# Moving the sum of the query rotation from VectorE to POOL in an attention and feed-forward kernel

## The chip, the cores and the metric

The kernel runs on one core of one Trainium2 chip. The metric is the device time of one execution in microseconds (us). Engines are called as in the profile: PE (TensorE), DVE (VectorE), ACT (ScalarE), POOL (GpSimd), SP (SyncE, which here only issues DMAs).

## The reference

Two sublayers, on an input of 2 batches, 1024 tokens and 512 features in float32:

```
q, k, v = projections of layernorm(x)          # 16 query heads, 4 key/value heads of 128
q = q * cos + rotate_half(q) * sin             # k too
q, k = elu(q) + 1, elu(k) + 1
state += k v^T ; z += k ; out = (q state) / (q z + 1e-6)     # causal linear attention
x = x + layernorm(out @ Wo.T)
h = silu(x' Wg) * (x' Wu), of each group of 4 only the 2 largest by size
x = x + layernorm(h @ Wd)                      # x' = layernorm(x)
```

What matters here is the second line: the rotated query is a sum of two products, `q * cos` and `rotate_half(q) * sin`.

## The kernel before

Every matrix is split into a high part (rounded to the matmul's format) and a low part (the rest), and every product of matrices is three matmuls: high by high, low by high, high by low (`three`, L383 to 386). ACT writes the high parts, and mostly POOL, at times DVE, the low parts by one subtraction. On POOL these all go through the helper `lo` and so have one line, L936; they are told apart by their tile.

The program is written out by hand as a row of ticks, the same for all engines (`TICKS`). Ticks -7 to 65 are the attention (`slot_a(s)` on each engine), the later ones the feed-forward part (`slot_f(n)`). A tick s from 0 to 63 handles one block of 128 tokens of one of the 8 units (batch by key/value head, four query heads each, 8 ticks to a unit). In it:

- PE, in this order: the values' product and the state's of block s-1 (`bank_o`, `bank_d`), the state update (`bank_st`), in every fourth tick (s a multiple of 4) a transpose of the values (`bank_t`, L465), the scores of block s (`bank_s`, L474), the output projection of block s-2 (`bank_y`), in every fourth tick a transpose of the keys (L489), and the query projection for a later block (`bank_q`), then keys or values for a later block in two ticks of four. Most ticks of the attention have 41 to 53 matmuls.
- DVE: in odd ticks the query rotation of two heads. Three instructions read the query bank in PSUM and write the products `M1` and `M2` (L754, L756, L758), and one adds them (L760, `M1 = M1 + M2`, 128x1024). Behind it in the same tick stand the state's low parts (L783, L784), the masking of the scores (L790, tile `Sf`) and the chain that divides (L801, L808, L813), which frees the banks that PE's next tick writes. In even ticks DVE begins with L764, which finishes elu + 1 of the rotated queries, and then does the rest.
- SP: in odd ticks `pair_rows` (L342 to 348) waits for the sum and issues four DMAs that bring the halves of two heads together (`M1` to `xq`, both in `scratch`).
- ACT: the high parts and exponentials. At the end of every odd tick it waits for those DMAs and computes `exp` and `relu` of the queries (L664, L665). Its weight splits (L602) stand behind them in its program. In ticks 1, 9, ..., 57 these are one query piece and the four pieces of the output weights (`wout_hi`).
- POOL: for each block the low part of the masked scores (`s_lo`), in one odd tick of two that of the keys (`k_lo`), then that of the attention result (`a_lo`), in even ticks that of the queries (`big_lo`, 128x1024), then the weights' (`w_lo`, `wout_lo`). In ticks 27 to 34 it also adds the residual rows (L953). Before all this come small steps of the layer norm (L941, L943).

The order within an engine is fixed, so an instruction that waits holds back everything behind it. The staging ring for weights has four places, and SP loads the next piece when the low part of the piece four before it is done. In eight ticks of the attention (3, 7, 11, 15, 39, 43, 47, 51) PE also transposes normalised input rows, last but for projections; DVE's low part of these (`x_lo`, L735) comes in the following tick right behind L764, and PE's transpose of the values in that tick (L465) waits for it.

Of the kernel before, what the change touches and what calls it, by code (L numbers as in the profile page):

```python
# [7 lines left out]
ALU = mybir.AluOpType  # L8
# [15 lines left out]
STEPS = UNITS * 2  # L24
# [128 lines left out]
def build(nc, x, wq, wk, wv, wo, wg, wu, wd, cos_t, sin_t, causal, eye, x1, out):  # L153
    with ExitStack() as ctx:
# [3 lines left out]
        def sem(name):  # L158
            return ctx.enter_context(nc.semaphore(name))
# [41 lines left out]
        M1, M2, xq = scr[:, 0:2, :], scr[:, 2:4, :], scr[:, 4:6, :]  # L201
# [56 lines left out]
        act_vt, act_vh = sem("act_vt"), sem("act_vh")  # L258
        act_qe, act_qh = sem("act_qe"), sem("act_qh")
        act_sth, act_ln, act_r0, act_sh, act_ah = [sem(n) for n in ("act_sth", "act_ln", "act_r0", "act_sh", "act_ah")]  # L260
        dve_q, dve_x, dve_f = sem("dve_q"), sem("dve_x"), sem("dve_f")
        dve_k1, dve_k2, dve_kx, dve_kf = sem("dve_k1"), sem("dve_k2"), sem("dve_kx"), sem("dve_kf")
        dve_stl, dve_s, dve_vl, dve_ktl = sem("dve_stl"), sem("dve_s"), sem("dve_vl"), sem("dve_ktl")
        dve_T, dve_U, dve_a, dve_y = sem("dve_T"), sem("dve_U"), sem("dve_a"), sem("dve_y")
# [15 lines left out]
        def rows_wait(gate, job):  # L280
            if job[0] == "in" and job[1] == 0:
                gate.wait_ge(ld_in[job[2]], 16)
            else:
                i = ROWS.index(job)
                gate.wait_ge(ld_row[i % RING_R], 16 * (i // RING_R + 1))
# [18 lines left out]
        def _(sp):  # L304
            g = Gate(sp)
# [34 lines left out]
                sp.dma_start(to[b, t * P:(t + 1) * P, :], xr[:, i % RING_R, :]).then_inc(st_row[i % RING_R], 16)  # L340

            def pair_rows(j):  # L342
                g.wait_ge(dve_x, j + 1)
                g.wait_ge(pool_fl, j)
                for h in range(2):
                    for a in range(2):
                        sp.dma_start(xq[a * HALF:(a + 1) * HALF, h, :],
                                     M1[h * HALF:(h + 1) * HALF, a, :]).then_inc(ld_xq, 16)
# [356 lines left out]
        def _(dve):  # L705
            g = Gate(dve)
# [37 lines left out]
            def slot_a(s):  # L744
                tick = tick_a(s)
                m, m2 = s - 1, s - 2
                if s % 2 and 0 <= s + 5 < 2 * STEPS * 2:
                    j = (s + 5) // 2
                    a = j // 2 % 2
                    g.wait_ge(tab_ld, 32)  # L750
                    g.wait_ge(pe_q, 2 * j + 2)
                    g.wait_ge(ld_xq, 64 * j)
                    g.wait_ge(dve_f, j)
                    dve.tensor_tensor(M1, psQ[:, :, :], cosb[:, a:a + 1, :].to_broadcast([P, 2, W]),  # L754
                                      ALU.mult).then_inc(dve_q, 1)
                    dve.scalar_tensor_tensor(M2[:, 0, :], psQ[:, 1, :], -1.0, sinb[:, a, :],  # L756
                                             ALU.mult, ALU.mult).then_inc(dve_q, 1)
                    dve.tensor_tensor(M2[:, 1, :], psQ[:, 0, :], sinb[:, a, :], ALU.mult).then_inc(dve_q, 1)  # L758
                    g.wait_ge(dve_q, 3 * (j + 1))
                    dve.tensor_tensor(M1, M1, M2, ALU.add).then_inc(dve_x, 1)  # L760
                if s % 2 == 0 and 0 <= s + 4 < 2 * STEPS * 2:
                    j = (s + 4) // 2
                    g.wait_ge(act_qe, j + 1)
# [167 lines left out]
        @block.gpsimd  # L931
        def _(pool):
            g = Gate(pool)

            def lo(dst, full, hi):
                return pool.tensor_tensor(dst, full, hi.bitcast(F32), ALU.subtract)  # L936

            def deviation(job):
                q = JOBS.index(job)
                g.wait_ge(dve_var, q + 1)  # L940
                pool.tensor_tensor(rstd[q % 4], mv[q % 4][:, 1:2], eps_ln, ALU.add).then_inc(pool_eps, 1)  # L941
                g.wait_ge(pool_eps, q + 1)
                pool.tensor_tensor(rstd[q % 4], rstd[q % 4], mhalf, ALU.pow).then_inc(pool_rs, 1)  # L943

            def split(k):
                hi_to, lo_to = dest(PLAN[k][0])
                g.wait_ge(act_wh, k + 1)
                lo(lo_to, stage[:, k % RING_W, :], hi_to).then_inc(pool_wl, 1)

            def add(job):  # L950
                rows_wait(g, job)
                g.wait_ge(dve_nm, JOBS.index(job) + 1)
                pool.tensor_tensor(rows_of(job), rows_of(job), Y[:, job[2], :], ALU.add).then_inc(pool_add, 1)  # L953

            def slot_a(s):
                tick = tick_a(s)
                m = s - 1
                for job in at(tick, norm_tick, LATER):
                    deviation(job)
                if 0 <= s < SLOTS:  # L960
                    g.wait_ge(act_sh, s + 1)
                    lo(Sl[:, :], Sf, Sh[:, :]).then_inc(pool_sl, 1)
                for p in range(STEPS):
                    if s == (4 * p - 1 if p else -5):
                        g.wait_ge(act_kh, p + 1)
                        lo(Kl[:, :], xk, Kh[:, :]).then_inc(pool_kl, 1)
                if 0 <= m < SLOTS:
                    g.wait_ge(act_ah, m + 1)
                    lo(Al[:, :, :].rearrange("p h t -> p (h t)"), Tn,
                       Ah[:, :, :].rearrange("p h t -> p (h t)")).then_inc(pool_al, 1)  # L970
                if s % 2 == 0 and 0 <= s + 4 < 2 * STEPS * 2:
                    j = (s + 4) // 2
                    part = slice(2 * (j % 2), 2 * (j % 2) + 2)
                    g.wait_ge(act_qh, j + 1)
                    lo(big_l[:, j // 2 % 2, part, :], xq, big_h[:, j // 2 % 2, part, :]).then_inc(pool_fl, 1)
                for k in pieces_at(tick, "qkvogu"):
                    if not by_dve(PLAN[k][0]):
                        split(k)
                for job in at(tick, lambda j: sum_tick(*j) + 1, ADDS):
                    add(job)  # L980

            def slot_f(n):
                tick = tick_f(n)
                for k in pieces_at(tick, "d"):
                    if not by_dve(PLAN[k][0]):
                        split(k)
                for job in at(tick, norm_tick, LATER):
                    deviation(job)
                if n % 4 == 0 and 4 <= n <= SLOTS:
                    d = n // 4 - 1  # L990
                    for i in range(2):
                        g.wait_ge(act_hh, 4 * d + i + 1)
                        lo(big_l[:, d % 2, i, :], hid[:, i, :], big_h[:, d % 2, i, :]).then_inc(pool_hl, 1)
                for k in pieces_at(tick, "gu"):
                    split(k)
                for job in at(tick, lambda j: sum_tick(*j) + 1, ADDS):
                    add(job)

            g.wait_ge(const_ok, 1)
            for t in range(4):  # L1000
                deviation(("in", 0, t))
            for k in pieces_at(-8, "kq"):
                split(k)
            for kind, i in TICKS:
                if kind == "a":
                    slot_a(i)
                else:
                    slot_f(i)
# [45 lines left out]
```

## Time and profile before

| | before |
|---|---|
| device time, median of 3 runs (lowest to highest) | 1338.29 us (1337.2 to 1342.01) |
| the profiled execution's own time | 1340.39 us |
| its span in the profile | 1338.6 us |
| mean granted TensorE clock | 0.982 |
| PE busy | 1245.9 us, 93% |
| DVE busy | 941.7 us, 70% |
| POOL busy | 672.0 us, 50% |
| ACT busy | 566.3 us, 42% |
| granted clock, 78 to 740 us (attention) | 1.00 |

The profile comes from one execution; its rows are compared with its own time. "Idle before" in a row is the time for which the engine had nothing to run, and behind the arrow stands who ended it. Granted clock 1.00 is 2.4 GHz, 0.50 is 1.2 GHz.

### The profile page before, as it was taken

How to read it: one execution, taken by the hardware profiler on the slowest of the kernel's cores; microseconds unless marked ns; L12 is line 12 of the kernel's file. 1: busy time of each engine (PE TensorE's matmuls, PEld its weight loads, DVE VectorE, ACT ScalarE, POOL GpSimd, SP SyncE). 2: the span in 40 equal slices, each digit the busy share in tenths (PEclk: the TensorE clock that was granted, in tenths of full speed). 3: DMA queues.
4: the chain of work that ended last, by engine and by line, in shares of the span. 5: the costliest groups of instructions: out<-in, count | busy, mean ns of one | idle time of the engine just before them, and what ended most of it. 6: DMA issues, size and time to landing. Idle time of an engine off the chain costs nothing.

```text
span 1338.6 us, 15339 instructions
## 1 busy us (share of the span) xinstructions
PE 1245.9 (93%) x5496; PEld 1005.8 (75%) x5496; DVE 941.7 (70%) x1426; ACT 566.3 (42%) x994; POOL 672.0 (50%) x524
## 2 busy tenths in 40 slices
PE   5679999999999999999998799999999999999995
PEld 4457777778778687787786577888888878888874
DVE  6458787877788878787877646667657765555576
ACT  3255555465555554645556333333323232323220
POOL 4156565554577765655645663434334643333316
PEclk9789999999999999999999899999999999999997
DMA  4232122122223222222121332212122322111103
GB/s 169 51 92 63 40 71 72 34 69 54 80 68 99 87 79 53 68 58 77 46 48 56 102 96 62 79 49 71 40 63 63 118 72 55 40 56 44 43 1 110
DMA packets 50059, 90.26 MB, mean 67 GB/s; under 512 B 6464, under 2 KB 6720, under 8 KB 49984
## 3 DMA queue, kind: packets, MB, share of 16 engines
q1 hardware_dynamic: 49984, 89.29, 23.5%
q8 instruction: 44, 0.72, 0.2%
q14 instruction: 31, 0.25, 0.1%
HBM read 64.09 MB, written 8.39 MB: 54 GB/s over the span
## 4 chain that ended last, share of the span: by engine, by line
PE 62%; DVE 18%; ACT 6%; issue 6%; DMA 3%; POOL 3%; SPq 1%; POOLq 0%; DVEq 0%; ACTq 0%
PE bank_q L384 6%; PE bank_q L386 6%; PE bank_q L385 6%; PE bank_o L384 3%; PE bank_t L384 3%; PE bank_t L386 3%; PE bank_t L385 3%; PE bank_o L386 3%; PE bank_o L385 3%; PE bank_s L384 3%; PE bank_s L386 3%; PE bank_s L385 3%; PE bank_d L384 2%; PE bank_d L386 2%; PE bank_d L385 2%
## 5 line engine op out<-in xcount | busy, mean ns | idle before, releaser
L936 POOL TENSOR_TENSOR big_lo<-scratch,big_hi 128x1024 fp32r<-128x1024 f32 (+1 forms) x64 | 150.4, 2359 | 231.5 <-ACT big_hi L688 217.1
L384 PE MATMUL bank_q<-x_hi,w_hi 128*128 128x512 f32 x448 | 180.3, 403 | 14.6 <-DVE scratch L758 7.9
L936 POOL TENSOR_TENSOR w_lo<-stage,w_hi 128x512 fp32r<-128x512 f32 x96 | 139.1, 1457 | 108.6 <-ACT w_hi L602 108.6
L386 PE MATMUL bank_q<-x_lo,w_hi 128*128 128x512 f32 x448 | 177.6, 397 | 0.0
L385 PE MATMUL bank_q<-x_hi,w_lo 128*128 128x512 f32 x448 | 177.4, 396 | 0.0
L936 POOL TENSOR_TENSOR s_lo<-scratch,s_hi 128x512 fp32r<-128x512 f32 x64 | 92.6, 1448 | 140.2 <-ACT s_hi L638 140.2
L679 ACT ACTIVATE scratch<-scratch 128x512 f32<-128x512 f32 x64 | 40.5, 632 | 233.4 <-DVE scratch L885 233.2
L936 POOL TENSOR_TENSOR a_lo<-scratch,a_hi 128x512 fp32r<-128x512 f32 x64 | 82.9, 1296 | 97.9 <-ACT a_hi L657 97.9
L384 PE MATMUL bank_y<-wout_hi,a_hi 128*128 128x512 f32 x256 | 103.6, 405 | 12.5 <-POOL wout_lo L936 8.5
L384 PEld LDWEIGHTS bank_q<-x_hi,w_hi 128*128 128x128 f32 x448 | 86.0, 192 | 33.8 <-POOL w_lo L936 7.0
L386 PE MATMUL bank_y<-wout_lo,a_hi 128*128 128x512 f32 x256 | 101.7, 397 | 0.0
L385 PE MATMUL bank_y<-wout_hi,a_lo 128*128 128x512 f32 x256 | 101.7, 397 | 0.0
L386 PEld LDWEIGHTS bank_q<-x_lo,w_hi 128*128 128x128 f32 x448 | 85.8, 192 | 18.8
L385 PEld LDWEIGHTS bank_q<-x_hi,w_lo 128*128 128x128 f32 x448 | 86.0, 192 | 17.9
L657 ACT CAST a_hi<-scratch 128x512 fp32r<-128x512 f32 x64 | 39.8, 621 | 125.5 <-DVE scratch L813 125.5
L764 DVE SCALAR_TENSOR_TENSOR scratch<-scratch 128x1024 f32<-128x1024 f32 x32 | 40.1, 1254 | 58.1 <-ACT scratch L665 58.1
L384 PE MATMUL bank_t<-x_hi,w_hi 128*128 128x512 f32 x192 | 75.6, 394 | 1.5 <-DVE x_lo L735 1.5
L688 ACT CAST big_hi<-scratch 128x512 fp32r<-128x512 f32 x64 | 39.2, 623 | 86.7 <-DVE scratch L857 76.2
L385 PE MATMUL bank_t<-x_hi,w_lo 128*128 128x512 f32 x192 | 75.4, 393 | 0.0
L386 PE MATMUL bank_t<-x_lo,w_hi 128*128 128x512 f32 x192 | 75.4, 393 | 0.0
L384 PEld LDWEIGHTS bank_y<-wout_hi,a_hi 128*128 128x128 f32 x256 | 48.3, 189 | 31.3 <-POOL wout_lo L936 12.7
L638 ACT CAST s_hi<-scratch 128x512 fp32r<-128x512 f32 x64 | 39.7, 621 | 63.5 <-DVE scratch L790 63.5
(233 smaller groups left out, 3402.3 us busy)
## 6 DMA issues: line engine op xcount, KB each, us to landing
scratch<-scratch SPq DMA_DIRECT2D x128, 128.0 KB, 2.3
x_rows<-x SPq DMA_DIRECT2D x56, 256.0 KB, 2.9
stage<-wq SPq DMA_DIRECT2D x32, 256.0 KB, 2.7
stage<-wo SPq DMA_DIRECT2D x32, 256.0 KB, 2.6
stage<-wg SPq DMA_DIRECT2D x32, 256.0 KB, 2.7
stage<-wu SPq DMA_DIRECT2D x32, 256.0 KB, 2.8
stage<-wd SPq DMA_DIRECT2D x32, 256.0 KB, 2.6
x<-x_rows SPq DMA_DIRECT2D x16, 256.0 KB, 2.4
```

The costliest lines, as they stand in the source:

```text
L384: pe.matmul(ps, whi, xhi, start=first, stop=False, skip_group_check=True)
L385: pe.matmul(ps, wlo, xhi, start=False, stop=False, skip_group_check=True)
L386: return pe.matmul(ps, whi, xlo, start=False, stop=last, skip_group_check=True)
L638: copy(Sh[:, :], Sf).then_inc(act_sh, 1)
L657: copy(Ah[:, :, :].rearrange("p h t -> p (h t)"), Tn).then_inc(act_ah, 1)
L679: act.activation(ab[:, i, :], hid[:, i, :], ACT.Abs).then_inc(act_ab, 1)
L688: copy(big_h[:, d % 2, i, :], hid[:, i, :]).then_inc(act_hh, 1)
L764: dve.scalar_tensor_tensor(xq, E, 1.0, xq, ALU.min, ALU.add).then_inc(dve_f, 1)
L936: return pool.tensor_tensor(dst, full, hi.bitcast(F32), ALU.subtract)
```

## The change

DVE's fourth rotation instruction goes, and POOL gets the same addition in its odd ticks, behind the low part of the scores and ahead of the low parts of keys and attention result. The semaphore that SP waits for now comes from POOL.

```diff
-        dve_q, dve_x, dve_f = sem("dve_q"), sem("dve_x"), sem("dve_f")
+        dve_q, pool_x, dve_f = sem("dve_q"), sem("pool_x"), sem("dve_f")
...
             def pair_rows(j):
-                g.wait_ge(dve_x, j + 1)
+                g.wait_ge(pool_x, j + 1)
                 g.wait_ge(pool_fl, j)
...
                     dve.tensor_tensor(M2[:, 1, :], psQ[:, 0, :], sinb[:, a, :], ALU.mult).then_inc(dve_q, 1)
-                    g.wait_ge(dve_q, 3 * (j + 1))
-                    dve.tensor_tensor(M1, M1, M2, ALU.add).then_inc(dve_x, 1)
...
                 if 0 <= s < SLOTS:
                     g.wait_ge(act_sh, s + 1)
                     lo(Sl[:, :], Sf, Sh[:, :]).then_inc(pool_sl, 1)
+                if s % 2 and 0 <= s + 5 < 2 * STEPS * 2:
+                    g.wait_ge(dve_q, 3 * ((s + 5) // 2 + 1))
+                    pool.tensor_tensor(M1, M1, M2, ALU.add).then_inc(pool_x, 1)
```

The condition holds in 32 ticks: -5, -3, -1 and the 29 odd ticks from 1 to 57.

POOL in ticks 17 and 18, before (`s_lo` opens a tick, `wout_lo` are the output weights' low parts, which are the last of tick 17):

```order
L936 TENSOR_TENSOR s_lo<-scratch,s_hi 128x512 [waits act_sh]
L936 TENSOR_TENSOR a_lo<-scratch,a_hi 128x512 [waits act_ah]
L936 TENSOR_TENSOR w_lo<-stage,w_hi 128x512 [waits act_wh]
L936 TENSOR_TENSOR wout_lo<-stage,wout_hi 128x512 [waits act_wh] x2
L936 TENSOR_TENSOR s_lo<-scratch,s_hi 128x512 [waits act_sh]
L936 TENSOR_TENSOR a_lo<-scratch,a_hi 128x512 [waits act_ah]
L936 TENSOR_TENSOR big_lo<-scratch,big_hi 128x1024 [waits act_qh]
```

and with the change (the helper's line is two lower, since two lines above it went):

```order
L934 TENSOR_TENSOR s_lo<-scratch,s_hi 128x512 [waits act_sh]
L963 TENSOR_TENSOR scratch<-scratch 128x1024 [waits dve_q]
L934 TENSOR_TENSOR a_lo<-scratch,a_hi 128x512 [waits act_ah]
L934 TENSOR_TENSOR w_lo<-stage,w_hi 128x512 [waits act_wh]
L934 TENSOR_TENSOR wout_lo<-stage,wout_hi 128x512 [waits act_wh] x2
L934 TENSOR_TENSOR s_lo<-scratch,s_hi 128x512 [waits act_sh]
L934 TENSOR_TENSOR a_lo<-scratch,a_hi 128x512 [waits act_ah]
L934 TENSOR_TENSOR big_lo<-scratch,big_hi 128x1024 [waits act_qh]
```

One instruction, L963, has come in between `s_lo` and `a_lo` of the odd tick; the even tick is as it was.

DVE in tick 17, before, from the three products of the rotation to the masking of the scores:

```order
L754 TENSOR_TENSOR scratch<-bank_q,scratch 128x1024 [waits dve_f,ld_xq,pe_q]
L756 SCALAR_TENSOR_TENSOR scratch<-bank_q,scratch 128x512
L758 TENSOR_TENSOR scratch<-bank_q,scratch 128x512
L760 TENSOR_TENSOR scratch<-scratch 128x1024 [waits dve_q]
L735 TENSOR_TENSOR x_lo<-bank_t,x_hi 128x4x128 [waits act_xh]
L783 TENSOR_TENSOR st_lo<-bank_st,st_hi 128x128 [waits act_sth]
L784 TENSOR_TENSOR st_lo<-bank_st,st_hi 128x128
L790 TENSOR_TENSOR scratch<-bank_s,mask 128x512 [waits pool_sl,pe_s]
```

In the change the row of L760 is gone and the others stand as they did. The sum therefore used to stand three rows ahead of L790; now it stands behind what follows from L790: the mask on DVE, `s_hi` on ACT, `s_lo` on POOL. PE's, ACT's and SP's rows are the same but for the semaphore.

## Rows read from the trace of the kernel before

**Rows 1.** The page, busy time of three engines over the whole run

```profile
PE 1245.9 (93%) x5496; PEld 1005.8 (75%) x5496; DVE 941.7 (70%) x1426; ACT 566.3 (42%) x994; POOL 672.0 (50%) x524
```

**Rows 2.** Waits, whole run: us in total, times, longest us

```profile
DVE scratch L764 <- ACT scratch L665: 58.1, 24, 6.2
...
PE bank_o L384 <- DVE scratch L813: 17.1, 15, 3.6
...
PE bank_t L465 <- DVE x_lo L735: 10.7, 8, 1.5
...
PE bank_y L384 <- POOL wout_lo L936: 8.5, 8, 1.4
```

**Rows 3.** Groups of instructions, 0 to 720 us: busy us, mean ns of one

```profile
L760 DVE TENSOR_TENSOR scratch<-scratch 128x1024 f32<-128x1024 f32 x32 | 62.0, 1939 | 1.1
...
L936 POOL TENSOR_TENSOR big_lo<-scratch,big_hi 128x1024 fp32r<-128x1024 f32 x31 | 74.5, 2403 | 14.3 <-ACT big_hi L653 14.2
...
L953 POOL TENSOR_TENSOR x_rows<-x_rows,y_acc 128x512 f32<-128x512 f32 x8 | 14.8, 1846 | 0.0
```

**Rows 4.** Timeline, tick 17 and tick 18: start, duration, instruction, idle before and releaser

```profile
263.96 2.27 DVE L760 TENSOR_TENSOR scratch<-scratch 128x1024 f32<-128x1024 f32 x1
...
266.26 2.38 SPq L347 DMA_DIRECT2D scratch<-scratch  x4
...
267.15 0.68 DVE L790 TENSOR_TENSOR scratch<-bank_s,mask 128x512 f32<-128x512 f32 x1
...
268.56 1.75 POOL L936 TENSOR_TENSOR s_lo<-scratch,s_hi 128x512 fp32r<-128x512 f32 x1 [3.41 <-ACT s_hi L638]
...
270.43 1.06 ACT L664 ACTIVATE scratch<-scratch 128x1024 f32<-128x1024 f32 x1
...
277.05 0.62 ACT L602 CAST wout_hi<-stage 128x512 fp32r<-128x512 f32 x1 [2.54 <-DMA stage<-wo]
...
279.08 0.50 PE L384 MATMUL bank_y<-wout_hi,a_hi 128*128 128x512 f32 x1 [0.79 <-POOL wout_lo L936]
```

**Rows 5.** Timeline, end of tick 21 and tick 22, and PE's first matmul of tick 23

```profile
310.30 2.39 SPq L347 DMA_DIRECT2D scratch<-scratch  x4
...
314.46 1.06 ACT L664 ACTIVATE scratch<-scratch 128x1024 f32<-128x1024 f32 x1 [0.49 <-DMA scratch<-scratch]
...
324.95 0.69 DVE L813 SCALAR_TENSOR_TENSOR scratch<-scratch,bank_o 128x512 f32<-128x512 f32 x1
...
329.01 0.40 PE L384 MATMUL bank_o<-s_hi,v_hi 128*128 128x512 f32 x1
```

**Rows 6.** Timeline, end of tick 11 and tick 12

```profile
201.86 1.74 POOL L936 TENSOR_TENSOR s_lo<-scratch,s_hi 128x512 fp32r<-128x512 f32 x1 [1.06 <-ACT s_hi L638]
...
205.04 1.05 ACT L664 ACTIVATE scratch<-scratch 128x1024 f32<-128x1024 f32 x1
...
208.22 0.68 DVE L735 TENSOR_TENSOR x_lo<-bank_t,x_hi 128x512 fp32r<-128x512 f32 x1
...
208.96 0.66 PE L465 MATMUL bank_t<-ident,scratch 128*128 128x128 f32 x4 [1.27 <-DVE x_lo L735]
```

**Rows 7.** Timeline, tick 23 and tick 24

```profile
334.33 1.29 POOL L936 TENSOR_TENSOR s_lo<-scratch,s_hi 128x512 fp32r<-128x512 f32 x1 [4.30 <-ACT s_hi L638]
...
337.45 1.05 ACT L664 ACTIVATE scratch<-scratch 128x1024 f32<-128x1024 f32 x1
...
342.03 0.69 DVE L790 TENSOR_TENSOR scratch<-bank_s,mask 128x512 f32<-128x512 f32 x1 [1.31 <-PE bank_s L386]
...
342.64 0.68 DVE L796 TENSOR_TENSOR v_lo<-bank_t,v_hi 128x512 fp32r<-128x512 f32 x1
...
344.62 0.60 PE L489 MATMUL bank_t<-ident,scratch 128*128 128x128 f32 x4
```

**Rows 8.** Timeline of PE, tick 60: one instruction

```profile
740.42 0.77 PE L384 MATMUL bank_o<-s_hi,v_hi 128*128 128x512 f32 x1 [3.60 <-DVE scratch L813]
```

**Rows 9.** Stretch of PE: its length, busy (instructions), granted clock, DMA share, GB/s

```profile
740.40:744.80 4.40, 4.38 (x10) 0.50 0.05 7
```

## The prediction

> **What bounds the kernel now.** I read the page first: PE is busy 93% of the span, DVE 70%, POOL 50% [rows 1]. By these averages DVE is the fuller of the two helpers and has work to give. But PE is the bound, so what counts is not how full DVE is but which wait PE ends on. That is the second view, the waits [rows 2]. PE waits for `x_lo` from DVE (10.7 us, 8 times), for `wout_lo` from POOL (8.5 us, 8 times) and for DVE's L813 (17.1 us, 15 times). None of these names the sum, L760. The row that leads to it is DVE's own: L764 waits 58.1 us in 24 of its 32 turns for ACT's `relu` of the queries, L665. That instruction comes from the chain sum, four DMAs, `exp`, `relu`, and both ACT and DVE stand still for it with everything behind them.
>
> Third view, the timeline of one pair of ticks. In tick 17 the sum ends at 266.23, SP issues at 266.26, ACT's `exp` starts at 270.43 [rows 4]. How long the DMAs take is best seen where ACT waited for them: issue at 310.30, `exp` at 314.46 with 0.49 us of waiting [rows 5], so 4.16 us from issue to `exp`. In tick 17 this gives 270.42, and `exp` starts at 270.43: no slack at all. Behind it ACT splits the output weights, the last at 277.05, after a DMA whose place in the ring is freed by the `w_lo` before; POOL makes `wout_lo` of it, and PE begins at 279.08 after a wait of 0.79 [rows 4]. So in this tick the sum is on the path that sets the end, by way of three engines and two sets of DMAs.
>
> **The change, part by part.**
>
> *DVE loses the sum.* 32 instructions of 1939 ns, 62.0 us [rows 3]. In odd ticks, what follows on DVE starts up to 2.27 us earlier (tick 17). PE gains only where L813 of an odd tick was its last wait. Of the 17.1 us in that row the largest is the 3.60 us ahead of tick 60 [rows 8], where there is no sum any more; most of the others end even ticks. I take a gain of 1 us, with ends at 0 and 17.1.
>
> *POOL gets it.* There is no row of this addition on POOL. The nearest is `big_lo`, of the same 1024 elements in float32: 2403 ns. From below, DVE's own time of 1.9 us; from above, twice the residual add of 512 elements, 2 x 1846 = 3.7 us [rows 3]. I take 2.4. POOL is half idle, so its busy time costs nothing in itself. The Trainium skill, page "GPSIMD Engine Reference", section 3.1, states 4497 ns for an add of 2048 float32 on this engine; an estimate of half of that is 2.25 us, with which the sum below would be some 3 us smaller. The row decides.
>
> *The place.* The sum no longer follows L758 at once. It stands behind `s_lo`, which needs L790 on DVE and `s_hi` on ACT. Tick 17: L760 is gone, so L790 and `s_lo` can move up by its 2.27 us, `s_lo` from 268.56 to 266.3. It takes 1.75 [rows 4], ends at 268.05, and the sum ends at 268.05 + 2.4 = 270.45 in place of 266.23. **The sum comes 4.2 us later**, and with it the DMAs and `exp`. Now class by class, since each pair of ticks closes on itself: the next rotation starts when PE's query projection is done, so lateness does not add up, but each stall of PE stays.
>
> - *Ticks 2, 10, ..., 58 (8), waiting for `wout_lo`.* No slack, as shown. ACT's splits, the load of the last piece and its low part move by the full amount: 8 x 4.2 = 34 us. DVE's divide chain of this tick stands behind the same splits and moves too, so nothing is caught up.
> - *The eight ticks after a row transpose in an odd tick (4, 8, 12, 16, 40, 44, 48, 52).* L465 waits for `x_lo`, which stands right behind L764: 208.96 with 1.27 us of wait already. In tick 11, `s_lo` (201.86) can move up by about 1, since POOL has two small steps ahead of it; with 1.75 and 2.4 the sum ends near 205, `exp` starts near 209.1 in place of 205.04 [rows 6], 4.0 later. 8 x 4.0 = 32 us.
> - *The other multiples of 4 (20, 24, 28, 32, 36, 56).* Here the keys' transposes wait for `v_lo`, behind L764. In tick 23 `s_lo` waits for PE's scores and does not move: 334.33 + 1.3, half a us for a DVE instruction that gets in between (`s_lo` took 1.29 here and 1.75 in tick 17), 2.4: 338.5. `exp` at 342.7 in place of 337.45, 5.2 late. DVE's wait of 1.31 ahead of L790 absorbs a part, the 1.3 us between `v_lo`'s end (343.32) and L489 (344.62) another [rows 7]: 2.6 is left. The other five have `exp` less late; I take 2.3 on average, 14 us.
> - *Ticks 6, 14, ..., 54 (7).* PE's tick 23 waits for L813 of tick 22, done at 325.64, needed at 329.01, slack 3.4 [rows 5]. Late by 4.3: 0.9 us, 7 us in all.
> - *Start, ticks -5 to -1.* Nothing else runs here, so each sum adds 2.4 - 1.94 = 0.5, and the third also stands behind a `big_lo`: 3 us in all, between 0 and 7.
>
> 34 + 32 + 14 + 7 + 3 - 1 = 89 us.
>
> *`k_lo` and `a_lo`*, behind the sum on POOL, move too. In tick 23 they would end at 338.5 + 1.8 + 1.3 = 341.6, and PE's scores of tick 24 end at 342.0 with the output projection next [rows 7]: covered, within some tenths. If the sum took 3.7 this cover would be gone and 1 us a time be lost in 14 ticks. *SP* has row loads and stores behind `pair_rows`; they move by the same 4 to 5 us, and are used a tick later: nothing.
>
> *The clock.* After a wait of 3.60 us [rows 8] PE ran 4.40 us at a granted 0.50, 1.2 GHz [rows 9]. Ten matmuls took that time, which at full clock take half: 2.2 us lost. The eight waits for `x_lo` become 1.3 + 4.0 = 5.3 us long. I charge these with 2.1 each, 17 us; in the `wout_lo` ticks the wait comes in pieces of up to 3 us, which I charge nothing. Ends: 0, and 22 times 2.1 = 46.
>
> Sum: 89 + 17 = 106. The profiled execution took 1340.4, so 1446; the median of the runs is 2.1 us lower: **1444 us**, 7.9% slower.
>
> **The rivals.**
> 1. *Half of it passes.* If the sum ends earlier than I reckon, or ACT and DVE catch up from their many small idle times, only the ticks without any slack pay: 34 + 3 = 37 us, 1375, up to about 1415 without the clock and the weaker classes. For it: DVE's lead grows by 2 us in odd ticks. Against: the two tight classes show no slack. 0.18.
> 2. *POOL and DVE get in each other's way.* L760 took 2.27 us when it met POOL's work and 1.94 on average. DVE instructions between SBUF tiles would now wait for a sum of 2.4 us, in place of doing it in 1.9, and DVE's relief is gone. With 0.5 us in each of 29 ticks more the time is 1444 + 15 = 1459, with clock drops in the `wout_lo` ticks 1476. The Trainium skill, "SBUF — State Buffer", section "SBUF: two separate sides", has it that the port pair of the two engines is an exclusive lock, held for a whole instruction; by that rule the offload speaks against itself. 0.08.
> 3. *Faster: DVE's relief decides.* Place: DVE's products on which PE waits, L813 and `x_lo`. If `exp` had slack of 4.2 us or more ahead of L764, the sum's lateness would be hidden and those waits would shrink by up to 1.9 us each: at most 10.7 + 5 (L813 in the 15 cases, less those that end even ticks) = 16 us, 1322. The point: the DMAs must have landed 4.2 us before ACT comes to `exp`. [rows 4, 5] show 0 and less. 0.07.
> 4. *No change*, 1338: the sum hides and there is no relief either, PE's order alone sets the pace. The 93% speak for it, the waits of rows 2 against. 0.05.
>
> **How the numbers follow.** My forecast, 1415 to 1470, has 0.62. The range reaches down to rival 1's lower end and up over half of rival 2: 1375 to 1470, which leaves about 0.12 below and 0.08 above. A measurement can tell 0.5%, 7 us, from no change. Faster by more: 0.07. Within: 0.05. Slower: 0.88.
>
> **What would show it.** The new POOL row: 32 instructions of about 2.4 us. DVE busy down by some 62 us, PE's nearly the same but for clock. Issue of the four DMAs 4 us later relative to L758. L764's wait for L665 up from 58 to 120 us or more. PE's waits for `x_lo` from 1.3 to about 5 us each, for `wout_lo` and its neighbours to 4 to 5 us a unit, a new wait of L489 for `v_lo`. Low clock after the `x_lo` waits. After tick 66 nothing changes. If L764's wait does not grow, the chain is wrong; if it grows and PE's do not, the slack is.

## The result, and the profile after

| | before | after |
|---|---|---|
| device time, median (lowest to highest) | 1339.49 us (1337.2 to 1342.01, 4 runs) | 1455.64 us (1451.41 to 1456.47, 4 runs) |
| ratio to before, 95% interval | | 1.0862 [1.0842, 1.0883] |
| span in the profile | 1338.6 us | 1454.6 us |
| mean granted TensorE clock | 0.982 | 0.949 |

The change costs 116 us, 8.6%, where 106 were forecast (1444 us; range 1375 to 1470). The line for before has one run more than the table ahead of the prediction.

The page after, busy time of the engines [rows 1 before], and one line of its fourth part (the chain that ended last, by engine):

```profile
PE 1286.2 (88%) x5496; PEld 1032.3 (71%) x5496; DVE 906.8 (62%) x1394; ACT 565.8 (39%) x994; POOL 735.0 (51%) x556
...
PE 48%; DVE 13%; POOL 13%; ACT 9%; issue 7%; DMA 6%; SPq 4%; POOLq 0%; DVEq 0%; ACTq 0%
```

DVE has lost 35 us of busy time, not the 62 of the sum: other DVE instructions between SBUF tiles have grown, half of that on L728, of which more below. POOL has gained 63. Neither is near a full share. PE has 40 us *more* busy time for the same 5496 instructions and yet a share of 88% in place of 93%: it ran slower, and it waited. DVE's share of the chain that ended last fell from 18% to 13%, and POOL, which had 3% of it, has 13%.

The waits after (us in total, times, longest us) [rows 2 before]:

```profile
ACT scratch L664 <- DMA scratch<-scratch: 162.8, 32, 13.6
...
DVE scratch L762 <- ACT scratch L665: 144.0, 24, 9.5
...
PE bank_o L384 <- DVE scratch L811: 34.2, 29, 4.5
...
PE bank_t L465 <- DVE x_lo L735: 33.1, 8, 4.3
PE bank_y L384 <- DVE wout_lo L742: 32.9, 11, 5.6
```

L762 is the old L764, L811 the old L813. The wait of DVE for `relu` went from 58.1 to 144.0 us. PE's wait for `x_lo` went from 10.7 to 33.1 in the same 8 places, that for the divide chain from 17.1 to 34.2. The output weights' low parts come from DVE (two of four pieces) and from POOL (the other two), so two rows belong together: before, 8.5 us on POOL's [rows 2] and on DVE's

```profile
PE bank_y L384 <- DVE wout_lo L742: 4.1, 6, 1.1
```

make 12.6 us; after, 32.9 on DVE's and 1.5 on POOL's make 34.4. All PE waits between the first and the last attention tick were some 39 us and are some 113.

Tick 17 and 18 in the timeline after [rows 4 before]:

```profile
298.95 0.68 DVE L758 TENSOR_TENSOR scratch<-bank_q,scratch 128x512 f32<-128x512 f32 x1
...
301.96 1.74 POOL L934 TENSOR_TENSOR s_lo<-scratch,s_hi 128x512 fp32r<-128x512 f32 x1 [2.01 <-ACT s_hi L638]
...
303.66 2.40 POOL L963 TENSOR_TENSOR scratch<-scratch 128x1024 f32<-128x1024 f32 x1
...
306.09 2.38 SPq L347 DMA_DIRECT2D scratch<-scratch  x4
...
310.23 1.06 ACT L664 ACTIVATE scratch<-scratch 128x1024 f32<-128x1024 f32 x1 [6.30 <-DMA scratch<-scratch]
...
314.78 0.47 PE L384 MATMUL bank_y<-wout_hi,a_hi 128*128 128x512 f32 x1 [3.10 <-DVE wout_lo L742]
...
316.38 0.80 PE L384 MATMUL bank_y<-wout_hi,a_hi 128*128 128x512 f32 x1 [0.65 <-DVE wout_lo L742]
...
316.93 0.62 ACT L602 CAST wout_hi<-stage 128x512 fp32r<-128x512 f32 x1 [2.62 <-DMA stage<-wo]
...
317.62 1.28 POOL L934 TENSOR_TENSOR wout_lo<-stage,wout_hi 128x512 fp32r<-128x512 f32 x1 [1.84 <-ACT wout_hi L602]
```

and the start of the same stretch in the kernel before:

```profile
263.24 0.68 DVE L758 TENSOR_TENSOR scratch<-bank_q,scratch 128x512 f32<-128x512 f32 x1
```

From the end of L758 to the issue of the DMAs it is 6.46 us (299.63 to 306.09); before it was 2.34 (263.92 to 266.26 [rows 4]). So the DMAs leave 4.1 us later (4.2 forecast), `exp` starts 4.14 us after the issue (4.16 read ahead), and behind it the last `wout_hi` comes after its load. PE's wait of 0.79 us for POOL's piece has become 3.10 + 0.65 for DVE's two; it takes up POOL's last piece, done at 318.90, without a wait, since the matmuls between ran slow (0.63 us each).

Tick 11 and 12 after [rows 6 before]:

```profile
224.86 2.84 POOL L963 TENSOR_TENSOR scratch<-scratch 128x1024 f32<-128x1024 f32 x1
...
225.37 2.62 DVE L728 TENSOR_SCALAR x_rows<-x_rows,small 128x512 f32<-128x512 f32 x1
...
228.73 0.47 PE L384 MATMUL bank_o<-s_hi,v_hi 128*128 128x512 f32 x1 [0.72 <-DVE scratch L811]
...
231.92 1.06 ACT L664 ACTIVATE scratch<-scratch 128x1024 f32<-128x1024 f32 x1 [2.68 <-DMA scratch<-scratch]
...
235.84 1.11 PE L465 MATMUL bank_t<-ident,scratch 128*128 128x128 f32 x4 [4.02 <-DVE x_lo L735]
...
238.46 0.63 PE L385 MATMUL bank_y<-wout_hi,a_lo 128*128 128x512 f32 x1
...
238.88 0.63 PE L386 MATMUL bank_y<-wout_lo,a_hi 128*128 128x512 f32 x1
...
241.01 0.39 PE L385 MATMUL bank_y<-wout_hi,a_lo 128*128 128x512 f32 x1
...
241.24 0.40 PE L386 MATMUL bank_y<-wout_lo,a_hi 128*128 128x512 f32 x1
```

Three readings. PE's wait for `x_lo` went from 1.27 to 4.02 us. After it the matmuls run 0.42 us apart (238.46, 238.88) and some 2 us later 0.23 (241.01, 241.24): 1.2 GHz, then 2.4 (the granted clock is 0.50 from 236.6 to 240.9 us and 0.99 in the 4.1 us behind). And DVE's L728, a layer-norm step that has nothing to do with the rotation, takes 2.62 us beside the sum on POOL, and the matmul at 228.73 waits 0.72 us for the divide chain behind it. At the same place before it took 1.52:

```profile
193.52 0.54 DVE L728 TENSOR_SCALAR x_rows<-x_rows,small 128x512 f32<-128x512 f32 x1
...
202.37 1.52 DVE L728 TENSOR_SCALAR x_rows<-x_rows,small 128x512 f32<-128x512 f32 x1
```

(timeline of the kernel before; the first of the two rows is the instruction undisturbed). The groups after, from 0 to 790 us, in which 30 of the 32 sums lie [rows 3 before]:

```profile
L963 POOL TENSOR_TENSOR scratch<-scratch 128x1024 f32<-128x1024 f32 x30 | 80.8, 2694 | 6.1 <-DVE scratch L758 6.1
...
L728 DVE TENSOR_SCALAR x_rows<-x_rows,small 128x512 f32<-128x512 f32 x16 | 25.2, 1577 | 0.0
```

The sum takes 2694 ns on average: some 2.4 us in ten of its 32 executions, as in tick 17, and 2.83 to 2.86 in twenty. L728 on rows went from 16 x 1025 to 16 x 1577 ns. The stretch of the attention and what follows (PE, PEld, DVE, ACT, POOL busy us, granted clock, DMA share, GB/s):

```profile
78.00:852.00 774.00, 668.02 (x2839) 529.45 (x2839) 490.49 (x705) 357.45 (x633) 442.38 (x304) 0.93 0.21 56
852.00:1454.00 602.00, 574.43 (x2502) 468.20 (x2500) 380.43 (x629) 184.42 (x327) 259.66 (x219) 0.98 0.22 65
```

Before, the attention's stretch was 662 us at 1.00, and 598 us followed it at 0.98: nearly all of the loss lies in the attention.

**Tick by tick.** Each attention tick begins with one matmul, the first of `bank_o`, so the distance from one to the next is the tick's length. Lengths after less lengths before, added up by the classes of the forecast:

| class of ticks | forecast, with its clock | measured |
|---|---|---|
| 2, 10, ..., 58 (`wout_lo`) | 34 | 34.5 |
| 4, 8, 12, 16, 40, 44, 48, 52 (`x_lo`) | 32 + 17 | 36.0 |
| 20, 24, 28, 32, 36, 56 (`v_lo`) | 14 | 20.3 |
| 6, 14, ..., 54 | 7 | 11.3 |
| odd ticks | -1 | 11.0 |
| start | 3 | 2.5 |
| the rest | 0 | 0.5 |
| sum | 106 | 116 |

Matmuls of 512 columns that took 0.55 us or more were 18 in the attention before and are 173. Each costs 0.42 - 0.23 = 0.19 us: 155 more are 30 us, a part of which PE would else have waited.

### The profile page after: what moved, and what is told of

Its sections match the earlier page's. It is cut to its first block, busy times and chain, and to the rows that moved or that the text cites. A ratio compares the mean times of both kernels' runs of the same rounds, so it can differ in the third digit from the quotient of the medians.

```text
span 1454.6 us, 15339 instructions
## 1 busy us (share of the span) xinstructions
PE 1286.2 (88%) x5496; PEld 1032.3 (71%) x5496; DVE 906.8 (62%) x1394; ACT 565.8 (39%) x994; POOL 735.0 (51%) x556
## 4 chain that ended last, share of the span: by engine, by line
PE 48%; DVE 13%; POOL 13%; ACT 9%; issue 7%; DMA 6%; SPq 4%; POOLq 0%; DVEq 0%; ACTq 0%
POOL scratch L963 5%; PE bank_q L384 5%; PE bank_q L385 5%; PE bank_q L386 5%; DMA scratch<-scratch 5%; SPq L347 3%; PE bank_o L384 3%; POOL s_lo L934 3%; PE bank_o L386 3%; PE bank_o L385 3%; PE bank_t L384 2%; PE bank_t L385 2%; PE bank_t L386 2%; PE bank_s L386 2%; PE bank_s L384 2%
## 5 line engine op out<-in xcount | busy, mean ns | idle before, releaser
L384 PE MATMUL bank_q<-x_hi,w_hi 128*128 128x512 f32 x448 | 183.3, 409 | 16.8 <-DVE scratch L758 10.6
L384 PE MATMUL bank_y<-wout_hi,a_hi 128*128 128x512 f32 x256 | 113.6, 444 | 34.8 <-DVE wout_lo L742 32.9
L934 POOL TENSOR_TENSOR s_lo<-scratch,s_hi 128x512 fp32r<-128x512 f32 x64 | 86.0, 1344 | 110.9 <-ACT s_hi L638 110.9
L762 DVE SCALAR_TENSOR_TENSOR scratch<-scratch 128x1024 f32<-128x1024 f32 x32 | 40.1, 1253 | 144.0 <-ACT scratch L665 144.0
L385 PE MATMUL bank_y<-wout_hi,a_lo 128*128 128x512 f32 x256 | 109.2, 427 | 0.0
L386 PE MATMUL bank_y<-wout_lo,a_hi 128*128 128x512 f32 x256 | 108.5, 424 | 0.0
L664 ACT ACTIVATE scratch<-scratch 128x1024 f32<-128x1024 f32 x32 | 33.9, 1059 | 162.8 <-DMA scratch<-scratch 162.8
L384 PEld LDWEIGHTS bank_y<-wout_hi,a_hi 128*128 128x128 f32 x256 | 53.8, 210 | 58.2 <-issue 34.2
L963 POOL TENSOR_TENSOR scratch<-scratch 128x1024 f32<-128x1024 f32 x32 | 86.1, 2690 | 6.1 <-DVE scratch L758 6.1
L806 DVE SCALAR_TENSOR_TENSOR scratch<-scratch 128x512 f32<-128x512 f32 x64 | 75.3, 1177 | 1.7
```

The costliest lines, as they stand in the source:

```text
L384: pe.matmul(ps, whi, xhi, start=first, stop=False, skip_group_check=True)
L385: pe.matmul(ps, wlo, xhi, start=False, stop=False, skip_group_check=True)
L386: return pe.matmul(ps, whi, xlo, start=False, stop=last, skip_group_check=True)
L664: act.activation(E, xq, ACT.Exp)
L762: dve.scalar_tensor_tensor(xq, E, 1.0, xq, ALU.min, ALU.add).then_inc(dve_f, 1)
L806: dve.scalar_tensor_tensor(Tn, Tn, 2.0, r0, ALU.subtract, ALU.mult).then_inc(dve_U, 1)
```

## The experiments

The theory: the sum is late because of its place behind `s_lo`, the DMAs and `exp` are late with it, and PE stops in the classes of ticks above. The rivals: POOL's work itself (its time, and the two engines in each other's way), DVE's lost order, or a loss that stands behind ACT's splits alone.

### The DMAs late, and nothing moved (e1_late_dmas)

The kernel before, DVE doing the sum; only SP waits longer, for the tick's `s_lo`.

```diff
                 g.wait_ge(dve_x, j + 1)
+                if 2 * j - 5 >= 0:
+                    g.wait_ge(pool_sl, 2 * j - 4)
```

> The sum stays on DVE, where it was; only SP waits, ahead of the four DMAs of an odd tick, for s_lo of that tick as well. No work moves. In tick 17 of before s_lo ends at 270.3 and the sum at 266.2, so the DMAs start 4.1 us later, as they do in the change. Theory of the late start (what counts is when the DMAs and exp start, not which engine adds): most of the loss comes back, 80 to 105 us over before, 1420 to 1445, with PE's waits for wout_lo and x_lo as long as in the change; less than the change itself by the odd ticks (11 us there) and the start (2.5 us). Rival, the engine itself is the cost (POOL's 86 us, and the two engines in each other's way): nothing moved, so within 10 us of before, 1330 to 1350.

Measured: 1424.37 us (1423.34 to 1426.12), ratio 1.0629 [1.0613, 1.0645]. Its waits (lines are two higher than before):

```profile
DVE scratch L766 <- ACT scratch L667: 127.3, 24, 6.2
...
PE bank_t L467 <- DVE x_lo L737: 32.7, 8, 4.3
...
PE bank_y L386 <- DVE wout_lo L744: 26.1, 11, 4.1
```

84.5 of the 116 us are here without one instruction on another engine. The `x_lo` class loses 35.4 us, as in the change (36.0), the `wout_lo` class 27.1, the `v_lo` class 14.7, the odd ticks only 2.6. The lateness is the cause of most. SP's loads of weights and rows stand behind the four DMAs in its order and are held back too, here as in the change; no run separates them from `exp`.

### The same work on POOL, in another place (e2_pool_sum_first)

The change, but with the sum ahead of `s_lo`.

```diff
-                if 0 <= s < SLOTS:
-                    g.wait_ge(act_sh, s + 1)
-                    lo(Sl[:, :], Sf, Sh[:, :]).then_inc(pool_sl, 1)
                 if s % 2 and 0 <= s + 5 < 2 * STEPS * 2:
                     g.wait_ge(dve_q, 3 * ((s + 5) // 2 + 1))
                     pool.tensor_tensor(M1, M1, M2, ALU.add).then_inc(pool_x, 1)
+                if 0 <= s < SLOTS:
+                    g.wait_ge(act_sh, s + 1)
+                    lo(Sl[:, :], Sf, Sh[:, :]).then_inc(pool_sl, 1)
```

> The change, but with the sum on POOL ahead of s_lo in its odd ticks. POOL adds as much as in the change. In tick 17 POOL is free at 265.2 (end of w_lo), so the sum ends near 267.6, 1.3 us later than on DVE, in place of 4.2. Theory of the late start: 8 x 1.3 in the wout_lo ticks, about 1 in half of the turn ticks, nothing in ticks that follow 7 mod 8, since exp had slack there: 10 to 25 us over before, 1345 to 1365. Rival, the engine itself is the cost: still at least 60 us over before, 1400 or more. Rival, DVE's relief is worth something once the sum is not late: below before, under 1333.

Measured: 1375.13 us (1371.61 to 1378.5), ratio 1.026 [1.0238, 1.0282]. Tick 17 of it:

```profile
271.00 0.68 DVE L758 TENSOR_TENSOR scratch<-bank_q,scratch 128x512 f32<-128x512 f32 x1
...
272.87 2.41 POOL L960 TENSOR_TENSOR scratch<-scratch 128x1024 f32<-128x1024 f32 x1
...
275.31 2.39 SPq L347 DMA_DIRECT2D scratch<-scratch  x4
...
279.46 1.06 ACT L664 ACTIVATE scratch<-scratch 128x1024 f32<-128x1024 f32 x1 [2.26 <-DMA scratch<-scratch]
```

From L758's end to the DMAs it is 3.6 us, between 2.3 and 6.4. Two POOL instructions in another order bring 80.5 of the 116 us back, though POOL does as much as in the change. It lies 10 us above the expected range. The `wout_lo` class came as reckoned (11.3 us, 10.4 expected); the `x_lo` class cost 10.7: ticks 4, 12, 44 and 52 lose 2.3 to 2.5 each, 8, 16 and 48 nothing, though in the tick before all of them the sum starts 1.4 us behind L758's end, after `big_lo` and two small layer-norm steps of POOL. What differs is PE: L758 ends 3.6 us into PE's tick before the four that lose and 0.7 before the three that do not, so there `x_lo` has 2.9 us more. And 5.0 came in odd ticks, 2.2 of them in tick 31.

### The work on POOL, without the lateness (e3_idle_adds)

The kernel before; POOL in addition adds 1024 elements in two instructions at the change's place. The target is the tile `Ek`, so ACT's `exp` of the keys must wait for the adds of the tick before as well (not shown in the cut); in the trace it never waits for POOL.

```diff
+                if s % 2 and 0 <= s + 5 < 2 * STEPS * 2:
...
+                    pool.tensor_tensor(Ek, cosb[:, 0, :], sinb[:, 0, :], ALU.add).then_inc(pool_d, 1)
+                    g.wait_ge(pool_d, s + 6)
+                    pool.tensor_tensor(Ek, cosb[:, 1, :], sinb[:, 1, :], ALU.add).then_inc(pool_d, 1)
```

> Before, and in addition POOL makes two adds of 512 elements at the place where the change has its sum, from the cosine and sine tables into a tile that is not in use, so its result goes nowhere. DVE still makes the real sum. Theory of the late start: only what stands behind on POOL moves (k_lo, a_lo) and DVE instructions between SBUF tiles are held up now and then: 0 to 15 us over before, 1338 to 1355. Rival, POOL's time and the two engines in each other's way are the cost: 60 us or more, 1400 and up.

Measured: 1358.49 us (1356.95 to 1359.27), ratio 1.0132 [1.0115, 1.0149]. So 18.6 us of the loss can come from POOL's occupation, 3.5 above my range. The places are in the queue behind the adds, in tick 17:

```profile
272.06 1.29 POOL L970 TENSOR_TENSOR scratch<-scratch 128x512 f32<-128x512 f32 x1
...
273.43 1.29 POOL L972 TENSOR_TENSOR scratch<-scratch 128x512 f32<-128x512 f32 x1
...
274.69 1.29 POOL L939 TENSOR_TENSOR a_lo<-scratch,a_hi 128x512 fp32r<-128x512 f32 x1
...
275.94 1.73 POOL L939 TENSOR_TENSOR w_lo<-stage,w_hi 128x512 fp32r<-128x512 f32 x1
...
282.29 0.50 PE L385 MATMUL bank_y<-wout_hi,a_hi 128*128 128x512 f32 x1 [1.90 <-POOL wout_lo L939]
```

`w_lo` frees a place of the staging ring, and comes later; the load of the last output piece waits for it, and PE with it (0.79 before, 1.90 here). In six even ticks PE waits for `a_lo`, 4.8 us in all, where it never did before. The change shows no wait for `a_lo`; why not is not shown. 18.6 and 84.5 are not two parts of 116 that may be added.

The odd ticks lose 0.3 us here, though POOL works as long in them as in the change. What differs is what the layer-norm step meets. In tick 11, beside `s_lo`:

```profile
203.36 1.51 DVE L731 TENSOR_SCALAR x_rows<-x_rows,small 128x512 f32<-128x512 f32 x1
```

It takes 1.51 or 1.52 us in ticks 3, 7, 11, 15, 27, 31, 39, 43, 47 and 51, as before and as in e1; in the change, where it starts 0.5 us behind the sum, 2.61 or 2.62 in each of them.

### ACT's splits ahead of `exp` (e4_change_splits_first, e5_before_splits_first)

If the `wout_lo` class loses because the splits stand behind `exp`, a swap on ACT must give it back. The edit in both kernels:

```diff
+                for k in pieces_at(tick, "qkvogud"):
+                    split(k)
                 if s % 2 and 0 <= s + 5 < 2 * STEPS * 2:
...
-                for k in pieces_at(tick, "qkvogud"):
-                    split(k)
```

> The change, with ACT's weight splits ahead of exp and relu of the queries in every tick. The weights' path no longer waits for the late DMAs: in tick 17 the splits can start at 304 in place of 312. Theory: the loss of the wout_lo ticks (34.5 us in the change) goes, and a little of the waits that were there before; exp itself starts 0 to 2 us later: 25 to 40 us below the change, 1415 to 1431. Rival, in these ticks DVE's divide chain behind exp is as late as the weights, so that moving the weights alone gives nothing: 1450 to 1460.

> The kernel before (sum on DVE), with ACT's weight splits ahead of exp and relu of the queries in every tick. Theory: in the wout_lo ticks PE's waits of before (12.5 us on the output projection) go, since the splits start some 2 us earlier, and at the start the wait for w_lo goes as it did with the same edit on the change (7.7 us there); against it exp starts later by one split of 0.5 us wherever it had no slack: 10 to 20 us below before, 1320 to 1330. Rival, exp is as tight here as the weights: the splits push it back in the wout_lo ticks and DVE's chain is later by as much as the weights are earlier, 1335 to 1345.

Measured: the change with it 1431.91 us (1430.39 to 1432.92), ratio 1.0683 [1.0667, 1.0699], 23.7 below the change. That is 0.9 us above the expected range. The `wout_lo` class went from 34.5 to 15.0 us: 19.5 of its loss stood behind `exp` through the splits. The start went from 2.5 to -5.2; this is a gain of the swap itself, since the kernel before has it too (7.0 us, next).

The kernel before with it: 1353.53 us (1351.51 to 1357.38), ratio 1.0103 [1.0085, 1.0121]: slower, and in neither expected range. Its tick 17:

```profile
270.25 1.66 ACT L602 CAST wout_hi<-stage 128x512 fp32r<-128x512 f32 x3
...
275.61 0.62 ACT L602 CAST wout_hi<-stage 128x512 fp32r<-128x512 f32 x1 [3.70 <-DMA stage<-wo]
...
276.14 1.06 ACT L666 ACTIVATE scratch<-scratch 128x1024 f32<-128x1024 f32 x1
...
278.17 1.23 DVE L764 SCALAR_TENSOR_TENSOR scratch<-scratch 128x1024 f32<-128x1024 f32 x1 [4.71 <-ACT scratch L667]
...
286.55 0.47 PE L384 MATMUL bank_o<-s_hi,v_hi 128*128 128x512 f32 x1 [1.97 <-DVE scratch L813]
```

PE no longer waits for `wout_lo`. But the last piece waits 3.70 us for its load, `exp` stands behind it, and PE pays through DVE's chain instead, which is what the rival said. The class ends at +2.2, and the odd ticks lose some 9 us more, mostly in 3, 11, 19, 35, 43 and 51, where 6 to 12 matmuls run slow behind such a wait; the `x_lo` class loses 7.5, and the start gains 7.0. With all splits moved, lateness of the weights has been traded for lateness of `exp`.

### A dose in between (e6_dmas_after_mask)

As the first experiment, but SP waits for the mask L790 of the tick, not for `s_lo`.

```diff
                 g.wait_ge(dve_x, j + 1)
+                if 2 * j - 5 >= 0:
+                    g.wait_ge(dve_s, 2 * j - 4)
```

> As the first experiment, but SP waits only for L790, the mask on DVE, of the same tick: a smaller dose of the same lateness. From the rows of before the DMAs start 1.6 us later in tick 17, 1.0 in ticks 11 and 21, 2.5 in tick 23 where 2.2 are slack. Theory of the late start, by class: 8 x 1.6 in the wout_lo ticks, some tenths in the others, with a little clock: 14 to 27 us over before, 1353 to 1367. Rival, the lateness only costs once it is past a threshold that the change passed: within 7 us of before.

Measured: 1354.09 us (1351.68 to 1354.57), ratio 1.01 [1.0081, 1.0118]; 9.1 us of it in the `wout_lo` class and 1 or less in each other. With this the price can be laid beside the lateness. Mean over 29 odd ticks, from L758's end:

| kernel | to the DMAs' issue | to `exp` | time against before | per us of `exp` |
|---|---|---|---|---|
| before | 2.05 us | 7.02 us | | |
| e6 | 3.38 | 7.65 | +14.4 us | 23 |
| e2 | 3.83 | 8.15 | +35.3 | 31 |
| e1 | 5.51 | 9.70 | +84.5 | 32 |
| the change | 6.50 | 10.66 | +116.2 | 32 |

e1 and the change lie on one line whether DVE or POOL adds. That POOL's own work adds nothing beyond the lateness that it makes is what this table suggests, but it does not show it, since the odd ticks differ. The price holds for these five alone, in which ACT's splits stand behind `exp`: with the splits ahead, `exp` came 9.00 us after L758 in e5 and 11.62 in e4, and the times were only 14 and 92 us above before (7 and 20 us per us).

### Three tries for a gain (e7_some_splits_first, e8_half_sums, e9_both)

What the fifth experiment taught: put ahead of `exp` only splits whose loads are there. On the kernel before:

```diff
+                pieces = pieces_at(tick, "qkvogud")
+                early = len(pieces) if s < 0 else len(pieces) - 1 if s % 8 == 1 else 0
+                for k in pieces[:early]:
+                    split(k)
                 if s % 2 and 0 <= s + 5 < 2 * STEPS * 2:
...
-                for k in pieces_at(tick, "qkvogud"):
+                for k in pieces[early:]:
```

> The kernel before, with ACT's weight splits ahead of exp only in the ticks below 0, and in ticks 1, 9, ..., 57 all but the last piece, the one that waits for its load. Theory: what made the full version slow was exp standing behind that last piece; with that piece behind exp again, the start keeps its 7 us and the wout_lo ticks gain 1 to 2 us each: 1315 to 1328. Rival, any delay of exp in the wout_lo ticks (here 2 us) comes back in DVE's divide chain: 1330 to 1345.

Measured: 1325.94 us (1325.12 to 1327.37), ratio 0.9891 [0.9876, 0.9907]: 13.5 us faster than the kernel before, and so faster than both. The start gives 4.8 and the `wout_lo` class 9.2. (The start is the least sure of these: it scatters by some 2 us between before, e1 and e6, in which it is the same program.) Its tick 17, 263 to 269 us:

```profile
263.35 1.66 ACT L602 CAST wout_hi<-stage 128x512 fp32r<-128x512 f32 x3
...
264.91 1.06 ACT L668 ACTIVATE scratch<-scratch 128x1024 f32<-128x1024 f32 x1
...
268.67 0.62 ACT L602 CAST wout_hi<-stage 128x512 fp32r<-128x512 f32 x1 [1.75 <-DMA stage<-wo]
```

The query piece and three of the output weights stand before `exp`, which follows them at once, and the piece whose load is late (1.75 us) stands behind it. On average `exp` starts 7.48 us after L758, 0.5 later than before, and the time is shorter all the same.

The eighth was meant to go the other way from the change: the DMAs earlier than before. DVE adds in two halves, and SP sends the first two DMAs after the first half.

```diff
-                g.wait_ge(dve_x, j + 1)
                 g.wait_ge(pool_fl, j)
-                for h in range(2):
-                    for a in range(2):
+                for a in range(2):
+                    g.wait_ge(dve_x, 2 * j + a + 1)
+                    for h in range(2):
...
+                    g.wait_ge(dve_q, 3 * j + 2)
+                    dve.tensor_tensor(M1[:, 0, :], M1[:, 0, :], M2[:, 0, :], ALU.add).then_inc(dve_x, 1)
                     dve.tensor_tensor(M2[:, 1, :], psQ[:, 0, :], sinb[:, a, :], ALU.mult).then_inc(dve_q, 1)
                     g.wait_ge(dve_q, 3 * (j + 1))
-                    dve.tensor_tensor(M1, M1, M2, ALU.add).then_inc(dve_x, 1)
+                    dve.tensor_tensor(M1[:, 1, :], M1[:, 1, :], M2[:, 1, :], ALU.add).then_inc(dve_x, 1)
```

> The kernel before, with the sum on DVE cut in two: the first half of M1 is added as soon as L756 is done, and two of the four DMAs start then; the other half and its two DMAs follow L758. The last DMA is issued about 1.1 us earlier. Theory of the late start, read backwards: 8 x 1 us in the wout_lo ticks and some in the turn ticks: 6 to 15 us below before, 1325 to 1334. Rival, 32 more instructions on DVE and the ports eat it: within 4 us of before.

Measured: 1344.64 us (1341.96 to 1346.8), ratio 1.0035 [1.0023, 1.0046]. That is 5.2 us above before, in neither expected range. The edit did not bring what it was made for. Counted from the start of the rotation (L754), since the first half sum puts L758 itself back, the DMAs left 0.4 us earlier in the 29 odd ticks from 1 to 57 (4.04 us in place of 4.44), and `exp` started 0.4 us *later* (9.80 in place of 9.44): ACT comes to it behind `a_hi`, which waits for DVE's chain, and the split instruction puts that chain back (in 18 of the 29 ticks ACT did not wait for the DMAs at all). The `wout_lo` class changed by 0.3, and 8.9 us were lost in odd ticks. In the start, where there is no such chain, `exp` came 3.1, 1.1 and 1.8 us earlier in the three rotations, and the start is 8.7 us shorter in the profiled execution (7.3 in the next run, against e7): there the earlier DMAs did pay. Three rows of tick 11:

```profile
189.12 1.75 DVE L759 TENSOR_TENSOR scratch<-scratch 128x512 f32<-128x512 f32 x1
...
191.50 0.69 DVE L762 TENSOR_TENSOR scratch<-scratch 128x512 f32<-128x512 f32 x1
...
196.69 0.47 PE L384 MATMUL bank_o<-s_hi,v_hi 128*128 128x512 f32 x1 [0.82 <-DVE scratch L815]
```

A half sum takes 0.69 us free (the second) and 1.75 beside POOL's `big_lo` (the first). The kernel with both edits:

> Both edits together. If both work they add up, since exp moves back by what the half sums gain: 1305 to 1322. If the first does nothing in the wout_lo ticks: about 7 us below the half sums alone.

Measured: 1327.45 us (1325.76 to 1330.41), ratio 0.9907 [0.9894, 0.9921]. No better than the seventh, and in neither of the two places expected (1305 to 1322, or some 7 us below the half sums alone; it is 17 below them): the odd ticks lose 8.8 us again, the `wout_lo` class gains 9.8.

## Why the prediction was right, point by point

- **The place decides.** Right. In tick 17 the DMAs left 4.1 us later, 4.2 by the reckoning, and `exp` came 4.14 us behind them. e1 shows 73% of the loss with no work moved, e2 gives 69% of it back with all work moved. That the forecast came within 10 us of the loss is in part luck: the `x_lo` term was 13 us too high, and the odd ticks, the `v_lo` class and the ticks 6, 14, ... were together some 23 us too low.
- **The price of the sum on POOL.** 2.4 us in tick 17, as taken; 2.69 on average. The estimate from the Trainium skill ("GPSIMD Engine Reference", section 3.1) was 2.25; the row of `big_lo` was nearer.
- **`wout_lo` ticks, 34 us.** 34.5. Charging no clock here was right for the sum though not in fact: 60 more matmuls ran slow in these ticks, but in tick 18 before the last piece had come (318.90 us, taken up at 319.11), so they cost time that PE would have waited. This is read from tick 18 alone. PE's long wait is not where I had it, at POOL's last piece, but at DVE's two; both stand behind the same `exp`.
- **`x_lo` ticks, 32 + 17 us.** 36.0, the term most overrated, by 13. PE's wait grew by 2.8 us each (33.1 less 10.7, over 8), not 4.0, and the clock took 64 x 0.19 = 12, not 17. In ticks 4, 12, 44 and 52 PE went on with the values' transpose 14.0 to 14.8 us behind L758's end, where it was 10.5 before, 3.4 in three of the four. But 0.7 of that had passed already: PE's tick began 6.9 us behind L758 (7.7 in tick 12) in place of 6.2, after the wait of some 0.7 us that ended the odd tick, and there it is counted. In 8, 16, 40 and 48 PE's tick began earlier against L758 than before (6.9 us, before 7.6 to 8.8); why is open.
- **`v_lo` ticks, 14 us, and 6, 14, ..., 54, 7 us.** 20.3 and 11.3. Of the first, 12.3 are PE's waits for `v_lo`, which it did not have in these ticks before, near the 14 forecast, and 18 slow matmuls are 3.4 more; no clock was charged there. Of the second, 4.7 is tick 30 alone, at whose end PE waited 4.51 us; with the sum on DVE and only the DMAs late (e1) this tick lost 4.4, and 4.3 in e2, so it is lateness too:

```profile
475.07 0.77 PE L384 MATMUL bank_o<-s_hi,v_hi 128*128 128x512 f32 x1 [4.51 <-DVE scratch L811]
```

- **DVE's relief, 1 us.** This step failed in its sign: the odd ticks lost 11.0 us. 3.2 are tick 31, with 11 slow matmuls behind the wait just shown; 7.3 stand in ticks 3, 7, 11, 15, 27, 39, 43, 47 and 51, 0.6 to 1.0 each. In each of them L728 met the sum and took 2.61 or 2.62 us, where it took 1.51 or 1.52 before, and PE waited at the tick's end for the divide chain behind it (0.71 to 0.73 us in eight of them, 1.15 in tick 27; before, at most 0.04 and 0.48). That is rival 2's mechanism, to which I had given 15 us in 29 ticks and a chance of its own; it came together with the forecast, in nine ticks. The page "SBUF — State Buffer" of the Trainium skill, section "SBUF: two separate sides", says that between a GpSimd operation and a VectorE operation that is in a 2-port perf mode (or has two SBUF inputs), whichever starts first holds the shared port pair for its whole length. No row here names the mode of L728, but its times agree with the rule: L728 began 0.51 us after the sum and took 2.62 less 0.54 = 2.08 us more than undisturbed, of the 2.33 that the sum still ran. That the meeting of L728 and the sum is what lengthens these nine ticks rests on these times, on e1, where POOL has no sum and the odd ticks lose 2.6 (1.2 of it tick 31), and on e3, where POOL works as long, L728 stays at 1.5 us and they lose 0.3. So it is not POOL's work as such, but that one instruction begins behind the sum.
- **The clock.** 30 us, not 17, though a part of it lies inside waits, as said. I had looked for it behind the waits for `x_lo` alone; 60 of the 155 slow matmuls stand in the `wout_lo` ticks and 29 in ticks 24, 31, 36 and 56.
- **The rivals.** DVE's wait rose to 144 us (120 or more forecast) and PE's with it, so neither half of the lateness passed (rival 1) nor did it hide (3, 4).

What stays open: how much of the last 32 us between e1 and the change is the 1 us more lateness and how much is POOL's occupation. Both kernels fit 32 us per us of `exp`, but the odd ticks (11.0 against 2.6) say that a part is the latter; the rest of the difference lies in the `wout_lo` class (7), the `v_lo` class (6), ticks 6, 14, ... (7) and the start (4), and no run divides it.

## What to carry to other kernels

When work is moved to an idle engine, its price is the place in that engine's order: find what stands ahead of it, and add that work's own releasers to the lateness of whatever the moved result starts. A DMA chain with no slack cost some 30 us for each us by which `exp` came later here, as long as ACT's splits stood behind it. What it gives when it comes earlier was not measured in the ticks: the one try moved `exp` earlier only in the start, which gained, and put it back elsewhere. So check in the trace that the consumer itself has moved, and count from an instruction that the edit leaves in place. A split of an order (some pieces ahead, the one with a late load behind) gained 1.1% where moving all of it lost 1.0%.

## What the runs showed of the hardware

- A `tensor_scalar` of 512 float32 between SBUF tiles on DVE took 0.54 us alone, 1.52 beside a POOL subtraction of 512 elements and 2.6 beside a POOL add of 1024, while the chain's instructions that read PSUM stayed at 0.68 us (L758, L811). The forecast had none of this for the instructions behind the sum; it stood in rival 2 alone.
- In the change, a wait of PE of 3.0 to 5.6 us in the middle of the attention was followed by 4 to 12 matmuls at 1.2 GHz in each of the 8 `x_lo` ticks and each of the 8 `wout_lo` ticks (in tick 34, 7 ran slow before the change too). Each of them took 0.19 us more.
- The add of 128x1024 float32 took POOL 2.40 us in tick 17 and 2.83 to 2.86 in 20 of 32 executions, where DVE took 1.94 on average [rows 3] for the same.
